# Two graph layers on one core: the stages of neighbouring graphs spread over the attention tiles as units that share two score bank pairs

## What is computed

```python
# x (16, 1024, 256) fp32, adj (16, 1024, 1024) int32 of 0 and 1
h = maximum(layernorm(x), 0)
Q, K, V = (h @ W.T + bias for the three weights), split in 8 heads of 32
scores = where(adj == 0, -inf, Q @ K.T / sqrt(32))
x = x + (softmax(scores) @ V, heads joined) @ Wo.T + bo
h = maximum(layernorm(x), 0)
e_k = leaky_relu((h * a_k) @ h.T, 0.2)          # k = 0..3
scores = e_0 where adj == 1, e_1 where adj == 2, ..., else -9e15
x = x + softmax(scores) @ h
```

## Time and profile before

| | us |
|---|---|
| three runs | 3979.12, 3986.06, 3994.07 |
| median | 3986.06 |
| profiled execution, first to last instruction | 3976.3 |
| TensorE busy | 3669.7 (92%) |
| VectorE busy | 3128.6 (79%) |
| ScalarE busy | 2267.1 (57%) |
| GpSimd busy | 674.9 (17%) |

### The profile page before, as it was taken

How to read it: one execution, slowest core, us unless ns; L and a number is a source line. 1 busy time by engine, 2 the same in 40 slices (tenths; PEclk the granted TensorE clock), 3 DMA queues, 4 the chain that set the end, 5 groups by cost and what they waited for, 6 DMA issues and landing times.

```text
span 3976.3 us, 94630 instructions
## 1 busy us (share of the span) xinstructions
PE 3669.7 (92%) x34096; PEld 2908.9 (73%) x34096; DVE 3128.6 (79%) x5926; ACT 2267.1 (57%) x3940; POOL 674.9 (17%) x440
## 2 busy tenths in 40 slices
PE   6989989899998989989899898998989989899998
PEld 5777777777777767777777777776777767777776
DVE  6968778687886978869788696886968869688785
ACT  3837547275573845738456384663836638366482
POOL 1021030310303103031020301203012030120300
PEclk8999999999999999999999999999999999999999
DMA  5041220403204032040310503104031040311300
GB/s 151 2 105 36 60 82 2 117 25 70 71 2 118 23 76 66 2 131 10 81 61 4 137 2 83 59 15 126 2 89 53 21 121 2 95 47 31 99 2 12
DMA packets 129070, 227.67 MB, mean 57 GB/s; under 512 B 20672, under 2 KB 71104, under 8 KB 128448
## 3 DMA queue, kind: packets, MB, share of 16 engines
q1 hardware_dynamic: 128448, 219.50, 20.3%
HBM read 101.98 MB, written 16.78 MB: 30 GB/s over the span
## 4 chain that ended last, share of the span: by engine, by line
PE 68%; SPq 11%; issue 9%; DVE 7%; DMA 2%; ACT 1%; DVEq 0%; POOL 0%; POOLq 0%; ACTq 0%
PE pT L856 21%; PE ps L837 15%; PE pO L873 13%; SPq L220 11%; PE ps L773 8%; PE pO L975 7%; PE pT L908 2%; DMA adj_half<-in_adj_dram 2%; PE pT L963 2%; DVE pt L525 1%; DVE most L483 1%; DVE sm L667 1%; PE pO L884 1%; DVE sm L510 1%; DVE sm L674 1%
## 5 line engine op out<-in xcount | busy, mean ns | idle before, releaser
L349 ACT ACTIVATE sm<-sm,mn 128x1024 f32<-128x1024 f32 x1024 | 1179.5, 1152 | 454.8 <-DVE mn L510 452.5
L510 DVE CUSTOM_DVE_ANT_0 sm<-ps,bias 128x1024 f32<-128x1024 f32 x1024 | 1250.9, 1223 | 197.5 <-PE ps L837 178.0
L856 PE MATMUL pT<-ident,sm 128*128 128x128 f32 x8192 | 1098.6, 276 | 40.3 <-DVE pt L525 37.1
L856 PEld LDWEIGHTS pT<-ident,sm 128*128 128x128 f32 x8192 | 961.3, 142 | 218.5 <-DVE pt L525 52.8
L837 PE MATMUL ps<-ks,qs 96*128 96x512 f32 x2048 | 754.4, 451 | 4.6 <-issue 3.7
L525 DVE COPY pt<-pT 128x512 f32<-128x512 f32 x1024 | 702.4, 686 | 31.5 <-PE pT L856 30.8
L873 PE MATMUL pO<-pt,v 128*32 128x128 f32 x16384 | 649.7, 278 | 4.8 <-DVE pt L525 4.8
L359 ACT COPY pt<-pT 128x512 f32<-128x512 f32 x1024 | 583.2, 570 | 56.7 <-PE pT L856 56.4
L290 POOL TENSOR_SCALAR bias<-adj_half 128x512 bf16<-128x512 int32 x240 | 468.0, 1950 | 864.3 <-DMA adj_half<-in_adj_dram 855.7
L873 PEld LDWEIGHTS pO<-pt,v 128*32 128x32 f32 x16384 | 388.2, 109 | 170.1 <-issue 170.1
L975 PE MATMUL pO<-h,pt 128*128 128x256 f32 x2048 | 463.0, 379 | 0.0
(11 more groups left out here) (104 smaller groups left out, 3526.5 us busy)
## 6 DMA issues: line engine op xcount, KB each, us to landing
adj_half<-in_adj_dram SPq DMA_DIRECT2D x256, 256.0 KB, 2.8
ks<-pt SPq DMA_DIRECT2D x384, 128.0 KB, 2.4
qs<-pt SPq DMA_DIRECT2D x384, 128.0 KB, 2.4
xf<-in_x_dram SPq DMA_DIRECT2D x16, 1024.0 KB, 8.0
x<-in_x_dram SPq DMA_DIRECT2D x16, 1024.0 KB, 5.7
out_dram<-x SPq DMA_DIRECT2D x128, 128.0 KB, 2.9
x<-in_L_gnn_Wq_dram SPq DMA_DIRECT2D x1, 256.0 KB, 2.8
x<-in_L_gnn_Wk_dram SPq DMA_DIRECT2D x1, 256.0 KB, 3.1
```

What stands on the lines that cost most here:

```text
L349: nc.scalar.activation(sm[:, t % RING, :], sm[:, t % RING, :], ACT.Exp, scale=-1.0, bias=mn[:, t:t + 1], accum_out=den[:, t:t + 1]).then_i ...
L510: nc.vector.tensor_tensor_reduce(out=sm[:, t % RING, :], in0=ps[t % 2][:, :], in1=bias[:, node, :], scale=1.0, scalar=3e38, op0=ALU.add, o ...
L856: last = nc.tensor.transpose(pT[c][:, j * P:(j + 1) * P], sm[:, t % RING, m * P:(m + 1) * P], ident[:, :])
```

## The change

**Stages.** `graph(b)` is replaced by `stage(b)`, which holds the 64 attention tiles of graph b, and between them units of its neighbours. A unit is one product or transpose of up to 1024 columns that fills one pair of the score banks `ps`, and that is read out of it by ScalarE and VectorE. `background` gives the tile after which each stands: the last Q part and the values of graph b itself (tiles 0, 1 and 4), the output product of graph b-1 (2 and 3), its h transposes (10 and 12), its eight edge scores (15, 18, ... 36), and for graph b+1 the transposes of its input (50 and 51) and three of its four Q and K parts (53, 54 and 61). Scores and units take the two bank pairs in turn (`score_banks`); which of them must have left a pair is what each waits for.

**Around the units.** The edge transposes of block t stand in tile 18 + 3t, and use `pT`; the product with h follows in two halves in the next two tiles. The value product of four tiles is issued in one piece, in every fourth tile, and no longer a quarter in each. `pO` becomes one bank `pA` for it and one bank `pB` for the rest.

**Work moved.** ScalarE does both layer norms with their relu (eight instructions each, in tiles 6, 7 and 48, 49) in place of GpSimd (first layer) and VectorE (second). The split lhs of the edge scores is made at once for 1024 columns from PSUM (`h_high`, `h_low`), and the additions after the output and value products take 1024 columns at a time. The mask of the second layer is a buffer of its own, `gbias`, for which `adj` is loaded a second time and made on GpSimd (`edge_bias`); so there are 32 loads of half a block for each graph, and not 16. The maxima for the flag (`most_kind`) stand on VectorE after tiles 36, 38, 41, 44, 48, 56, 63 and 6. The 48 small DMAs stand in two groups of 24: heads 0 to 3 after tile 54 of the stage before, heads 4 to 7 at the start of their own stage.

The diff, cut:

```diff
+def background(earlier, later):
+    units = {0: ("qk", 3), 1: ("value", 0), 4: ("value", 1)}
+    if earlier:
+        units.update({2: ("out", 0), 3: ("out", 1), 10: ("h", 0), 12: ("h", 1)})
+        units.update({15 + 3 * t: ("edge", t) for t in range(NT)})
+    if later:
+        units.update({50: ("front", 0), 51: ("front", 1), 53: ("qk", 0), 54: ("qk", 1), 61: ("qk", 2)})
+    return units
+def score_banks(units):
+    slots, turn = {}, 0
+    for s in range(TILES):
+        slots["score", (s + 2) % TILES] = turn % 2
+        turn += 1
+        if s in units:
+            slots[units[s]] = turn % 2
+            turn += 1
+    return slots
...
+            def load_adj(g, t, loaded):
+                for c in range(2):
+                    sp.wait_ge(adj_used[c], loaded)
+                    settle(sp)
+                    sp.dma_start(adj_half[:, c, :],
+                                 adj_t[g, t][:, c * HALF:(c + 1) * HALF]).then_inc(adj_in[c], 16)
...
+            def mask_adj(f, node, base):
+                if node == 0:
+                    sp.wait_ge(g_sel, 7 * (NT * (f - 2) + NT))
+                    settle(sp)
+                if node:
+                    sp.wait_ge(most_made, LOADS * f + 2 * node)
+                    settle(sp)
+                load_adj(f, node, base + NT + node)
...
+            def stage(b, later):
+                o, base = b - 1, LOADS * b
+                sp.wait_ge(s_mm, TILES * b)
+                settle(sp)
+                second_stacks(b, 0)
+                sp.wait_ge(most_made, LOADS * b + 2 * (NT - 1))
+                settle(sp)
+                load_adj(b, NT - 1, base - 1)
+                second_stacks(b, 1)
+                sp.wait_ge(most_made, LOADS * (b + 1))
...
+                if later:
+                    mask_adj(b + 1, 2, base)
+                    sp.wait_ge(pv, NT * (o + 1))
+                    settle(sp)
+                    load_xf(b + 1, 0)
+                    load_xf(b + 1, 1)
+                store(o, 7)
+                sp.wait_ge(y_out, 16 * NT * (o + 1))
+                settle(sp)
+                load_x1(b)
+                if later:
+                    mask_adj(b + 1, 3, base)
+                    mask_adj(b + 1, 4, base)
+                    mask_adj(b + 1, 5, base)
+                    sp.wait_ge(s_mm, TILES * b + TILES // 2)
+                    settle(sp)
+                    first_stacks(b + 1, 0)
+                    first_stacks(b + 1, 1)
+                    mask_adj(b + 1, 6, base)
...
+            def next_masks(f, node):
+                pool.wait_ge(masked, TILES * (f - 1) + TILES // 2 + HG * (node + 1))
+                masks(f, node, LOADS * (f - 1) + NT + node)
...
+            def stage(b, later):
+                o, base = b - 1, LOADS * b
+                next_masks(b, NT - 1)
+                layer_rstd(o)
+                for t in range(NT):
+                    edge_bias(o, t, base + t)
+                if later:
+                    for node in range(3):
+                        next_masks(b + 1, node)
+                    front_rstd(b + 1)
+                residual(b)
+                if later:
+                    for node in range(3, NT - 1):
+                        next_masks(b + 1, node)
...
+            def h_high(o, k, i):
+                act.wait_ge(l_tr, KT * o + k + 1)
+                nc.scalar.copy(hh[:, k, :], ps[i][:, :]).then_inc(l_h, 1)
+                if k == 0:
+                    for h in range(HG, H):
+                        act.wait_ge(k_stacked[h], STK * (o + 2))
+                        act.wait_ge(q_stacked[h], STK * (o + 2))
+                nc.scalar.activation(ah[:, k, :], ps[i][:, :], ACT.Copy, scale=nacol[:, 0, k:k + 1]).then_inc(a_h, 1)
...
+            def h_low(o, k, i):
+                dve.wait_ge(a_h, KT * o + k + 1)
+                nc.vector.tensor_tensor(hl[:, k, :], ps[i][:, :], hh[:, k, :].bitcast(F),
+                                        ALU.subtract).then_inc(l_l, 1)
+                nc.vector.scalar_tensor_tensor(out=al[:, k, :], in0=ps[i][:, :], scalar=nacol[:, 0, k:k + 1],
+                                               in1=ah[:, k, :].bitcast(F), op0=ALU.mult,
+                                               op1=ALU.subtract).then_inc(a_l, 1)
...
+                for s in range(TILES):
+                    if s + 2 < TILES:
+                        mask(b, s + 2, banks["score", s + 2], not earlier, made)
+                    elif later:
+                        mask(b + 1, s + 2 - TILES, banks["score", s + 2 - TILES], False, base + NT)
+                    kind, n = units.get(s, ("", 0))
...
+                    if kind == "edge":
+                        select(o, n, banks["edge", n], base + n, general)
+                        edge_mask(o, n, banks["edge", n], base + n)
...
+                    copy(b, s, not earlier)
+                    if kind == "edge":
+                        edge_leaky(o, n)
+                    if s % 16 == 15:
+                        row_factors(b, s // 16, not earlier)
+                    if kind == "out":
+                        layer_stats(o, n)
+                    if earlier and s == 3:
+                        layer_aggregate(o)
+                    if earlier and s == 5:
...
+                    if later and s in (45, 46):
+                        front_stats(b + 1, s - 45)
+                    if later and s == 46:
+                        front_aggregate(b + 1)
+                    if later and s == 47:
+                        front_shift(b + 1)
+                    if s == 52:
+                        flag_cell(b)
+                    if earlier and s == 6:
+                        most_kind(NT - 1, base - 1)
+                    if not earlier and s % 4 == 1 and s < 4 * (NT - 1):
+                        most_kind(s // 4 + 1, s // 4 + 1)
+                    if later and s in (36, 38, 41, 44, 48, 56, 63):
+                        node = (36, 38, 41, 44, 48, 56, 63).index(s)
+                        most_kind(node, base + NT + node)
...
+                for s in range(TILES):
+                    if s + 2 < TILES or later:
+                        if s - 1 in units:
+                            pe.wait_ge(masked, TILES * b + s + 2)
+                        elif s - 2 in units:
+                            released(b, units[s - 2])
+                        else:
+                            pe.wait_ge(masked, TILES * b + s + 1)
+                        if s + 2 < TILES:
+                            scores(b, s + 2, banks["score", s + 2])
+                        else:
+                            scores(b + 1, s + 2 - TILES, banks["score", s + 2 - TILES])
...
+                    if earlier and 18 <= s < 18 + 3 * NT and s % 3 == 0:
+                        pe.wait_ge(pt_made[0], TILES * b + s)
+                        pe.wait_ge(pt_made[1], TILES * b + s)
+                        edge_transposes(o, (s - 18) // 3)
+                    kind, n = units.get(s, ("", 0))
+                    if kind and s and s - 1 in units:
+                        released(b, units[s - 1])
+                    elif kind:
+                        pe.wait_ge(masked, TILES * b + s + 2)
+                    if kind == "value":
+                        value(b, n, banks["value", n])
...
+                        edges(o, n, banks["edge", n], general)
...
+                    if earlier and 19 <= s < 19 + 3 * NT and s % 3:
...
+                        edge_values(o, (s - 19) // 3, (s % 3 - 1,))
+                    if s == 1 and earlier:
+                        values(o, GROUPS - 1, False)
+                        pe.wait_ge(flag_made, b)
+                        pe.wait_ge(normed, QUADS * b - 1)
+                        rows(o, QUADS - 1)
+                    if s > 1 and s % HG == 1:
+                        values(b, s // HG - 1, not earlier)
+                    if s > 1 and s % 16 == 1:
+                        if earlier and s > 17:
+                            pe.wait_ge(y_made, NT * o + (5 if s == 33 else 8))
+                        if s > 17 or earlier:
+                            pe.wait_ge(normed, QUADS * b + s // 16 - 1)
+                        rows(b, s // 16 - 1)
...
+                    if earlier and 18 <= s < 18 + 3 * NT and s % 3 == 0:
+                        pe.wait_ge(lpt[0], NT * o + (s - 18) // 3 + 1)
+                        pe.wait_ge(lpt[1], NT * o + (s - 18) // 3 + 1)
+                    transposes(b, s, not earlier)
```

1439 lines of the change are left out of this document (744 added, 695 removed).

## The result

The changed kernel takes 4341.7 us (median of four runs, 4336.4 to 4346.3), the kernel before 3986.5 in the same comparison: a ratio of 1.090 [1.0875, 1.0919]. The profiled execution has a span of 4344.4 us. The forecast was 4135 with a range of 3800 to 4290. The sign was right, the size was not: the change costs 355 us, and the sum had 149.

A forecast was written before the change was run, and what follows sets the result against it. TensorE bounds the tiles, with VectorE only 0.34 us behind. Stretches summed to a period of 255 us, 9.2 above 245.8; 3976.3 + 14 x 9.2 + 20 = 4125 profiled, 4135 as median, range 3800 to 4290.

The forecast's parts named there:

- the sum: Whole kernel: 3976.3 + 14 x 9.2 + 20 = 4125 us for the profiled execution, 4135 as the median.
- Plain tiles: Tiles without a unit or value product: VectorE sets the pace, at 1.76 us each.
- 18 to 38: The stretch of tiles with edge blocks: seven triples at 13.5 us and `rows`, 95 us.
- (a): After tile 44 the maximum waits about 3 us for the load of block 3, issued behind the input and x.
- (b): After tile 48 the maximum waits 8.7 us for block 4, whose buffer waits for GpSimd's bias addition and mask.
- the seams of the earlier trace: Kernel before, second layer: time lost before the edge scores, for the split lhs, some 10 us a graph.
- The clock ... I count nothing: Whole graph: a steadier clock would give at most 4 us a graph, and no clock effect was counted.
- Tiles 6 to 14: Nine tiles at 1.76 us, two value products, two reads of h, one pair of maxima: 28 us, ScalarE's norms inside.
- The tail: Last layer of graph 15, alone after the stage: 8 blocks at about 8.4 us each, tail 92 us.
- Units: In VectorE-paced tiles the copy and next transposes wait for the unit's whole chain: about 4 us on top.
- Rival 1: Faster: TensorE queues ahead better, most waits close, period 228 us near the floor, time 3757 us; chance 0.27.
- Rival 3: Slower: the 24 small DMAs run into tile 0 or block 6's load is late; ten us gives 4275; chance 0.08.

The follow-up runs named there:

- experiment 1: Changed kernel, with the tail's loads of `adj` for block t issued ahead of the store of block t-2: 4292.1 us, ratio 1.0774.
- experiment 2: Changed kernel, with two stages in the loop body, so seven turns in place of fourteen: ratio 1.0816.
- experiment 3: Changed kernel, with ScalarE's second-layer norms two in each of tiles 6 to 9, not four in 6 and 7: ratio 1.0800.
- experiment 7: Changed kernel, with four units moved and keeping their bank pair longer while the next two scores take the other pair: ratio 1.1036.
- experiment 6: Changed kernel, with the tile's own transposes and copies ahead of every unit except the edge scores: ratio 1.1298.
- experiment 5: Changed kernel, with GpSimd's bias addition to x moved behind the masks of blocks 3 to 6: ratio 1.0702.
- the best version: The run with five edits, with GpSimd's bias addition between the masks of blocks 4 and 5 and input norms three, three, two a tile: 4099.4 us.
- the run with five edits: Changed kernel with bias addition behind masks, tail loads ahead of the store, norms two a tile, two stages a turn, later maxima: ratio 1.0361.

## Why the prediction was right and where it was wrong

**Direction, right, by its own reason.** Spreading moves units into tiles whose pace VectorE sets, where VectorE cannot use TensorE's room. Plain tiles are at 1.74 us (forecast 1.76), 18 to 38 at 95.0 us (95), the waits at the maxima at 2.65 us for (a) (3) and 8.1 for (b) (8.7). What the seams of the earlier trace rows gave back was less than what the new waits took. The size failed: the profiled execution is 219 us above the 4125 of the sum. Four steps of it are to blame; experiments 1 to 3 take back 50, 32 (for half of the turns) and 41 us of them.

**"The clock ... I count nothing": wrong.** The mean granted clock fell from 0.967 to 0.925. I argued from tiles in which TensorE had always been busy, and named (b) as new idle time without following it up. The stretches with new idle time ran at 0.79 to 0.94 on the mean. The clock alone takes 1.2 us at tiles 39 to 41 (14.2 on the mean against 13.0 in the stages at full clock), some 2 behind a turn (5.8 less 3.8 of standing) and up to 1.8 at tiles 6 to 14: an estimate of 4 to 5 of the 11.5 us a stage that were missed.

**The loop turn: left out.** It costs 3.8 us of standing and with the clock behind it 5.8 us on the mean (experiment 2). The kernel before pays 2.8 us for it, on VectorE. My stretches were built up from TensorE's work, so they needed a term for all of it; at 13 turns of 5.8 us that is 75 us.

**Tiles 6 to 14, a term put at nothing.** Four norms hold a tile 2 us and not 1, the sum of 28 held neither, and the clock comes on top: 31.5 and not 28 (experiment 3).

**The tail, term mis-sized.** 15 us a block and not 8.4. The step priced the block's own chain and had nothing for the load of `adj` that stands behind the store of the block before on SyncE's queue (experiment 1). That is 46 of the 60 us by which the tail was missed.

**Units, right in size, wrong in mechanism.** 3.5 to 4 us above the tile came out near the 4 forecast, but not for the turnover of the banks. Experiment 7 took that away and experiment 6 moved the copy out of the chain, and neither made a unit cheaper. That the number fits is luck. The rule of the Trainium skill that I weighed (Perfetto Trace Analysis, Matmuls: rotate independent groups through the banks) would have given 20 us by my estimate. In the one form in which it was tried here, it gave 0.5 us in tiles 10 to 14 and nothing at the Q and K parts, while the new places lost 5.4 us.

**Wait (b), right in size, half of it another thing:** VectorE's stretched instruction (experiment 5). This too is luck. The forecast said that VectorE idles some 11 us a graph for the DMA; the page of the kernel after has 102.3 us in all, 6 to 7 us a graph.

**Rivals.** Rival 1, whose ground was that TensorE had two graphs' work to choose from, is refuted by the trace: each engine's order is fixed, and two tiles of look-ahead are all that it can use. Rival 3's mechanism was not seen in the changed kernel: the small DMAs come in time. It appeared in experiment 7, at 6.4 us.

**What stays open.** What sets the clock in tiles 39 to 41 in one stage and not in the next; part of the loss in experiment 6; the 1 us each in tiles 15 to 17 and 50 to 54; and the 6 us a graph by which the best version (period 251.9) is still above 245.8. The grouping of the value product, which alone costs the kernel before at least 7 us a graph, is a rival for these that no run tests.

## What to carry to other kernels

Before work is spread into a loop, ask in each tile how far ahead the producer may run. With a look-ahead of two tiles, a unit cost the sum of TensorE's and VectorE's time for it here, although both have idle time elsewhere. New waits on TensorE have to be priced with the lower clock that may stand behind them (here up to 2 us more behind waits of 2 to 4 us), a loop's turn by the engine that it now stops, an instruction of VectorE with two SBUF inputs by what GpSimd does beside it, and a moved load by the place in the queue in which it now stands.

## What the runs showed of the hardware

- A VectorE instruction with two inputs in SBUF (L696, L700 in the run with five edits) took 4.79 us in place of 0.69 when it started behind a GpSimd addition of 4.56 us, and ended 0.55 us behind it. Which of the two starts first decides who is held. In the run with five edits, VectorE's instruction starts with the addition at 1509.01 and is held; at 3548.02 it starts 0.05 us ahead and keeps its time, and the addition takes 5.10 us:

```profile
1509.01 5.13 DVE L700 SCALAR_TENSOR_TENSOR ot<-mn,rden 128x512 f32<-128x512 f32 x1
1509.01 4.59 POOL L390 TENSOR_TENSOR x<-x,bob 128x2048 f32<-128x2048 f32 x1
...
3548.02 0.69 DVE L700 SCALAR_TENSOR_TENSOR ot<-mn,rden 128x512 f32<-128x512 f32 x1
3548.07 5.10 POOL L390 TENSOR_TENSOR x<-x,bob 128x2048 f32<-128x2048 f32 x1
```

- The loop's turn stopped TensorE for 3.2 to 4.5 us at the 13 turns of the kernel after, with no wait on any semaphore that the profile shows. In the kernel before it stopped VectorE for about 3 us (2.88 at 555.99) and TensorE's marker matmul came no later for it.
- The value product of 64 records took 1.96 us at full clock and 3.06 behind two waits of 2 us, where the granted clock from 1079.4 to 1090.0 us is 0.68.
- The same 119 matmuls took 10.81 us of TensorE at a granted clock of 1.00 and 12.45 at 0.88.
